# Local attention with the values as the stationary operand of four column groups and the mask in row tiles

## The chip, the cores and the metric

The kernel runs on one core of a Trainium2 chip. The metric is the device time of one execution in microseconds, the median over several runs. TensorE multiplies matrices from SBUF into PSUM, VectorE (DVE) and ScalarE (ACT) read and write both memories, GpSimd (POOL) works on SBUF only, and SyncE (SP) issues the DMAs. The engines run their own instruction streams and wait for each other by semaphores.

## The reference, cut to what matters

Two transformer blocks with adaptive layer norm run over x of shape (4, 1024, 256). The change touches only the attention of the first block, a local one with 16 heads of 16 channels and a window of 64 keys:

```python
h, w, dh, p = 16, 64, 16, 32
q = (x @ Wq.T).reshape(b, l, h, dh)
xp = jnp.pad(x, ((0, 0), (p, p), (0, 0)))
k = (xp @ Wk.T).reshape(b, l + 2 * p, h, dh)
v = (xp @ Wv.T).reshape(b, l + 2 * p, h, dh)
win_idx = jnp.arange(l)[:, None] + jnp.arange(w)[None, :]
scores = jnp.einsum('blhd,blwhd->blhw', q, k[:, win_idx]) * dh ** -0.5
attn = jax.nn.softmax(scores, axis=-1)
out = jnp.einsum('blhw,blwhd->blhd', attn, v[:, win_idx]).reshape(b, l, d)
return out @ Wo.T + bo
```

Query l sees keys l to l + 63 of the padded sequence. Four more stages follow: a latent attention, a mixture of experts, a rotary attention and a second mixture of experts. The change leaves them alone.

## The kernel before, in words

`windowed_attention` (L448) handles 4 batches of 1024 tokens. Each batch has 16 windows (NWIN) of 64 queries; a window needs the 128 keys around its queries, so 64 slots s = 0 to 63 of the main loop stand for the windows of all batches, and w is the slot's place in its batch. The 16 heads go in 8 pairs of 32 channels: the query tile `qm` holds each pair's 64 queries twice, once with the first head's channels and once with the second's (the others zeroed by `parity`), so one matmul per pair gives 128 rows (two heads by 64 queries) of 128 keys.

A window passes through these steps:

- `score` (L820): the mask `bandb` (bf16, 128 x 128) goes into the four PSUM banks of `S` by an identity matmul, one per bank (L827). Then eight matmuls of 32 rows each add the scores (L834), the four row tiles of the array in turn, each into its own bank. A plain fp32 matmul shows as two instructions in the trace, so there are sixteen.
- `softmax` (VectorE, L579): the row maximum of all 1024 columns (L581), then the subtraction into `D` (L585). The next window's `score` waits for the subtraction (`shifted`), since `S` is there once. ScalarE takes the exponential (L750).
- `turn_p` (L840): eight transposes of `D` (L846), copied to `PTs` by ScalarE (L757).
- `weigh` (L850): per pair the transposed weights `PTs` are the stationary operand (128 columns) and the pair's 32 value channels with two columns of ones move (34 columns, L862). Row sums come out beside the values. Both heads' rows meet both heads' channels, and only half of the products is wanted.
- `normal_out` (VectorE, L589): reciprocal of the sums (L592), its masking by `own` (L594), and the product that scales the values and zeroes the unwanted half (L599) into `Yn`.
- `lay` (L866): a selector product with `sel` folds the two heads' rows together and transposes (L871). `lay_out` (VectorE, L603) copies the result to `yT` (L608).

Odd windows read the values from `Vodd`, a copy of `V` shifted by 64 tokens, that two DMAs on SP's queue make per batch (L523, L524).

Beside the windows go **turns**: pieces of work on one shared PSUM bank. Those of a batch's preparation are four transposes of the normalised input ("turn"), four projections each for "query" and "key" (six fp32r matmuls of 512 columns, L799) and five for "value" (L809); ScalarE empties them. An "out" turn is the output projection of four windows (eight instructions of 256 columns, L816); VectorE adds the bias (`output`, L618), and GpSimd multiplies by the gate and adds to x (L694, L697). For the first batch the preparation comes ahead of the loop. For the others, and for all outputs, `WindowPlan` (L399) gives each slot at most two turns, and all of them use one bank, `PJ`. In a slot TensorE goes through this order (end of `windowed_attention`, L884 on):

```python
turn_p(s); lay(s - 2); score(s + 2); turn_bank(turns[0]); weigh(s - 1); turn_bank(turns[1])
```

and VectorE through `lay_out(s - 2)`, `softmax(s + 2)`, `normal_out(s - 1)`, then in slots 0 to 5 of batches 0 to 2 a piece of the next batch's layer norm (four BN_STATS in w = 0, four and eight aggregations in w = 1, four normalisations L576 in each of w = 2 and 3, two low parts `tokens_low` L626 in each of w = 4 and 5), then `output` where the slot has an out turn. An out turn for windows up to 4u + 3 stands in slot 4u + 6 (OUT_AT), as the first turn of its slot; the preparation begins in w = 3.

Of the kernel before, what the change touches and what calls it, by code (L numbers as in the profile page):

```python
# [14 lines left out]
P = 128  # L15
# [383 lines left out]
class WindowPlan:  # L399
# [9 lines left out]
    OUT_AT, FIRST_AT = 6, 3  # L409
    FIRST_BANKS = 6  # L410

    def __init__(self):
# [3 lines left out]
        self.slots = {}  # L416
        for s in range(B * NWIN + 3):
            b, i = divmod(s - self.OUT_AT, 4)
            out = [("out", b // 4, b % 4)] if i == 0 and 0 <= b < 4 * B else []
            self.slots[s] = out  # L420
        for b in range(1, B):
            s = (b - 1) * NWIN + self.FIRST_AT
            for kind, u in self.HEAD:
                while len(self.slots[s]) >= 2:
                    s += 1
                self.slots[s].append((kind, b, u))
        for s in sorted(self.slots):
            for turn in self.slots[s]:
                self.take(turn, self.FIRST_BANKS)
# [18 lines left out]
def windowed_attention(nc, sems, X, MODT, ROWS, ident, identb, eps, W, K):  # L448
    plan = WindowPlan()
    SLOTS = B * NWIN  # L450
    with ExitStack() as ctx:
# [8 lines left out]
        band, bandb = sb("band", [P, P]), sb("bandb", [P, P], BF16)  # L460
        parity = sb("parity", [P, 2])
        own = sb("own", [P, 2])
        sel = sb("sel", [P, WINDOW])
# [11 lines left out]
        V = sb("V", [P, 2, TT + 1, PAIRS, 34])  # L475
        Vodd = sb("Vodd", [P, 2, TT, PAIRS, 34])
# [3 lines left out]
        r = sb("r", [P, 2, PAIRS])  # L480
        rm = sb("rm", [P, 2, PAIRS, 2])
        Yn = sb("Yn", [P, 2, PAIRS, 2, A_DH])
# [7 lines left out]
        Y = O[:, 3 * P:3 * P + KC * WINDOW]  # L490
# [10 lines left out]
        recip, normal, laid, laid_out = signal("recip"), signal("normal"), signal("laid"), signal("laid_out")  # L501
# [10 lines left out]
        def _(sp):  # L512
# [6 lines left out]
            def odd_values(b):  # L519
                sp.wait_ge(freed_a, plan.after(("value", b, 4)))  # L520
                if b >= 2:
                    sp.wait_ge(weighed, NWIN * (b - 1))
# [11 lines left out]
            for dst, src in ((parity, K["parity"]), (band, K["band"]), (own, K["own"]), (sel, K["sel64"])):  # L534
                sp.dma_start(dst[:, :], src).then_inc(wload, 16)
# [22 lines left out]
        def _(v):  # L558
# [1994 lines left out]
```

## Time and profile before

| | us |
|---|---|
| median of three runs | 3053.94 |
| lowest, highest | 3047.06, 3055.08 |
| the profiled execution's own time | 3045.3 |
| its span | 3043.5 |

The profiler records one execution. A span is the time from its first to its last instruction. TensorE is busy for 86% of it, its weight loads for 70%, VectorE for 57%, ScalarE for 41%, GpSimd for 25%. A group of instructions is named by line, engine, operation and tiles; local attention's tiles begin with `w_`. Busy times of TensorE's matmuls overlap, so that the distance from start to start says what an instruction costs in a stream. "x16" is a run of sixteen merged into one row. In brackets stands how long the engine was idle before, and what released it. The granted clock (PEclk) is a share of full speed.

### The profile page before, as it was taken

The numbers are of one execution on the slowest core, as the hardware profiler recorded it, in microseconds if no ns is written. First come the engines' busy times: TensorE is split into PE (matmuls) and PEld (weight loads), VectorE is DVE, ScalarE is ACT, GpSimd is POOL, SyncE is SP. The second block draws the span as 40 slices with busy tenths as digits, with TensorE's granted clock in tenths as the row PEclk, the third lists the DMA queues.
The fourth block names the chain that finished last, engine by engine and source line by source line (L and its number), as shares of the span: only waits on it lengthen the run. The fifth ranks groups of instructions, "written<-read, shape, count | busy, mean of one in ns | idle before, by whom it ended". The sixth has DMA issues, their size and how long they took to land. (4 is left out here: it accounts for less than half of the span.)

```text
span 3043.5 us, 42168 instructions
## 1 busy us (share of the span) xinstructions
PE 2623.1 (86%) x15448; PEld 2115.3 (70%) x15448; DVE 1749.3 (57%) x3153; ACT 1248.0 (41%) x1815; POOL 763.3 (25%) x858
## 2 busy tenths in 40 slices
PE   4699998378999899999999939999587666899998
PEld 3588887256777777777777738888455444788887
DVE  3556655257767776687667625665323334666664
ACT  0444443136666566656666623332122113323322
POOL 0011101324343434353433211111133332100100
PEclk8899999679999999999999969999798887999999
DMA  3200100234333333433334222100100003000000
GB/s 119 81 26 24 28 26 15 68 99 120 102 97 109 107 102 98 134 92 103 106 109 112 76 83 77 37 30 15 68 14 16 29 29 116 8 23 8 30 8 15
DMA packets 127091, 194.59 MB, mean 64 GB/s; under 512 B 34864, under 2 KB 93104, under 8 KB 122224
## 3 DMA queue, kind: packets, MB, share of 16 engines
q1 hardware_dynamic: 125104, 191.50, 21.0%
q8 instruction: 118, 1.93, 0.3%
q10 hardware_dynamic: 1792, 0.53, 0.1%
q14 instruction: 77, 0.63, 0.1%
HBM read 118.28 MB, written 61.34 MB: 59 GB/s over the span
## 5 line engine op out<-in xcount | busy, mean ns | idle before, releaser
L1251 DVE TENSOR_REDUCE l_negmax<-l_mx 128x1 f32<-128x512 f32 (+3 forms) x608 | 393.7, 653 | 144.6 <-PE l_mx L1600 143.9
L1481 ACT ACTIVATE l_Phi<-l_s 128x1024 fp32r<-128x1024 f32 x288 | 295.1, 1025 | 263.6 <-PE l_s L1620 252.1
L1263 DVE TENSOR_TENSOR l_Plo<-l_s,l_Phi 128x1024 fp32r<-128x1024 f32 x288 | 349.7, 1214 | 13.5 <-ACT l_s L1485 12.8
L1631 PE MATMUL l_o<-l_Phi,l_V 128*128 128x256 f32 x1152 | 309.0, 290 | 7.0 <-ACT l_Osb L1493 2.2
L1618 PE MATMUL l_s<-l_QA,l_KK 128*128 128x512 f32 x576 | 284.6, 494 | 27.3 <-DVE l_Plo L1263 22.7
L1631 PE MATMUL l_o<-l_Plo,l_V 128*128 128x256 f32 x1152 | 302.2, 284 | 0.0
L1600 PE MATMUL l_mx<-l_KK,l_QA 128*128 128x512 f32 (+3 forms) x768 | 274.7, 398 | 29.3 <-DMA l_QB<-l_qd 15.9
L1485 ACT ACTIVATE l_s<-l_s 128x1024 f32<-128x1024 f32 x288 | 295.3, 1025 | 0.0
L2255 ACT ACTIVATE m_hidhi<-m_h 128x512 fp32r<-128x512 f32 x168 | 106.2, 632 | 458.0 <-DVE m_h L2113 458.0
L1631 PEld LDWEIGHTS l_o<-l_Phi,l_V 128*128 128x128 f32 x1152 | 221.6, 192 | 43.0 <-issue 31.7
L1620 PE MATMUL l_s<-l_QB,l_KL 65*128 65x512 f32 x576 | 230.8, 401 | 0.0
L1631 PEld LDWEIGHTS l_o<-l_Plo,l_V 128*128 128x128 f32 x1152 | 220.9, 192 | 13.2
L2358 PE MATMUL m_a<-m_wdhi,m_hidhi 128*128 128x256 f32 x672 | 214.5, 319 | 4.8 <-DVE m_tmp L2098 4.5
L1395 POOL TENSOR_TENSOR l_Y<-l_Osb,l_R 64x512 f32<-64x512 f32 x128 | 163.8, 1280 | 175.5 <-DMA l_R<-l_rd 166.6
L2358 PE MATMUL m_a<-m_wdhi,m_hidlo 128*128 128x256 f32 x672 | 189.9, 283 | 0.0
L2358 PE MATMUL m_a<-m_wdlo,m_hidhi 128*128 128x256 f32 x672 | 189.3, 282 | 0.0
L2117 DVE TENSOR_TENSOR m_hidlo<-m_h,m_hidhi 128x512 fp32r<-128x512 f32 x168 | 120.3, 716 | 107.4 <-ACT m_hidhi L2255 107.4
L2105 DVE TENSOR_TENSOR m_sg<-m_sg,m_c 128x512 f32<-128x512 f32 x128 | 87.7, 685 | 161.2 <-PE m_c L2346 143.5
L1600 PEld LDWEIGHTS l_mx<-l_KK,l_QA 128*128 128x128 f32 x768 | 143.3, 200 | 48.8 <-DMA l_QB<-l_qd 18.5
L1376 POOL TENSOR_TENSOR l_rp<-l_rp,l_cos 128x256 f32<-128x256 f32 x64 | 46.8, 732 | 492.2 <-DMA l_rps<-l_rp 481.1
L1618 PEld LDWEIGHTS l_s<-l_QA,l_KK 128*128 128x128 f32 x576 | 111.4, 193 | 61.0 <-DVE l_Plo L1263 40.4
L2205 POOL TENSOR_TENSOR m_xb<-m_xb,m_tmp 128x256 f32<-128x256 f32 x64 | 54.7, 871 | 342.1 <-DVE m_tmp L2098 339.6
(344 smaller groups left out, 6049.1 us busy)
## 6 DMA issues: line engine op xcount, KB each, us to landing
l_qd<-l_qs SPq DMA_DIRECT2D x256, 128.0 KB, 2.4
l_QA<-l_qd SPq DMA_DIRECT2D x64, 512.0 KB, 4.5
l_QB<-l_qd SPq DMA_DIRECT2D x64, 256.0 KB, 5.2
l_R<-l_rd SPq DMA_DIRECT2D x128, 128.0 KB, 3.0
l_rps<-l_rp SPq DMA_DIRECT2D x128, 64.0 KB, 1.9
m_xb<-xs SPq DMA_DIRECT2D x8, 1024.0 KB, 4.8
w_Vodd<-w_V SPq DMA_DIRECT2D x8, 544.0 KB, 5.6
w_xb<-in_x SPq DMA_DIRECT2D x4, 1024.0 KB, 6.1
```

The source lines that it names most:

```text
L1251: v.tensor_reduce(negmax[:, n % 2, at + h0:at + h1], piece_of(number, chunk), AX.X, ALU.max, negate=True).then_inc(reduced, 1)
L1263: v.tensor_tensor(Plo[:, s % 3].rearrange("p u h q -> p (u h q)"), S2[s % 2][:, :], Phi[:, s % 3].rearrange("p u h q -> p (u h q)").bitcas ...
L1395: g.tensor_tensor(Y[rows, quad % 2, 2 * grp:2 * grp + 2].rearrange("p j t q -> p t j q"), Osb[rows, r % 3, :, odd * 2 * P:(odd + 1) * 2 * ...
L1481: a.activation(Phi[:, s % 3].rearrange("p u h q -> p (u h q)"), S2[s % 2][:, :], ACT.Exp, scale=L_D ** -0.5).then_inc(exped, 1)
L1485: a.activation(S2[s % 2][:, :], S2[s % 2][:, :], ACT.Exp, scale=L_D ** -0.5).then_inc(exped, 1)
L1600: mm = pe.matmul(bank[:, h - h0, :], QA[:, n % 4, h, t, :], KK[:, b % 2, k0 * P:k1 * P], start=not diagonal, stop=(h == h1 - 1), skip_grou ...
L1618: pe.matmul(bank, KK[:, b % 2, k * P:(k + 1) * P], QA[:, m % 4, :, t, :], start=not diagonal, stop=False, skip_group_check=diagonal)
L1620: pe.matmul(bank, KL[:, b % 2, k * P:(k + 1) * P], QB[:, m % 4, :, t, :], start=False, stop=True, skip_group_check=diagonal).then_inc(scor ...
L1631: mm = pe.matmul(O[:, odd * 2 * P:(odd + 1) * 2 * P].rearrange("p (j q) -> p j q", j=2), V[:, b % 2, k, 64 - 64 * odd:192 - 64 * odd], src ...
L2117: v.tensor_tensor(hidlo[:, n % 3, :], h[:, n % 2, :], hidhi[:, n % 3, :].bitcast(F32), ALU.subtract).then_inc(low, 1)
L2255: a.activation(hidhi[:, n % 3, :], h[:, n % 2, :], ACT.Copy).then_inc(high, 1)
L2358: mm = pe.matmul(acc[q // 2][:, (q % 2) * C:(q % 2 + 1) * C], x[:, n % 3, q * P:(q + 1) * P], w[:, j, :], start=(j == 0 and q % 2 == 0 and ...
```

## The change

The values become the stationary operand. For each pair, `weigh` loads the pair's 32 value channels (32 columns) and streams the 128 columns of `PTs`, so that the output comes already transposed, channels on partitions. The four pairs of a group go to the four column groups of the array and write partitions 0 to 31, 32 to 63, 64 to 95 and 96 to 127 of the bank `O`. A second set of matmuls with 32 columns of ones gives the sums, spread over the same partitions. That makes 16 matmuls, 32 instructions, per window. `normal_out` picks each channel's own head by `parity` in two passes over 256 columns, takes the reciprocal of the 128 sums of each partition, and multiplies 128 elements into `yT`. `lay`, `lay_out`, `Yn`, `own` and `sel` are gone, and with them one slot of delay.

The mask goes in as eight matmuls of 32 rows: `hot` has the rows' one-hot of the query within each half of 32 queries, `pen` the penalties. `V` and `Vodd` lose the columns of ones. An out turn stands one slot earlier (OUT_AT 5) and is last in its slot. So slot 5 is (query, out) where it was (query, key), 6 is (key, query) where it was (out, query), 9 is (key, out), 10 and 11 are (value, value), 12 is (value), 13 and 17 are (out) alone, and likewise 16 slots on.

```diff
-    OUT_AT, FIRST_AT = 6, 3
+    OUT_AT, FIRST_AT = 5, 3
     FIRST_BANKS = 6
 
     def __init__(self):
         self.index, self.bank, self.order = {}, {}, []
         for n, (kind, u) in enumerate(self.HEAD):
             self.take((kind, 0, u), n % self.FIRST_BANKS)
-        self.slots = {}
-        for s in range(B * NWIN + 3):
-            b, i = divmod(s - self.OUT_AT, 4)
-            out = [("out", b // 4, b % 4)] if i == 0 and 0 <= b < 4 * B else []
-            self.slots[s] = out
+        last = {self.OUT_AT + 4 * n: ("out", n // 4, n % 4) for n in range(4 * B)}
+        self.slots = {s: [] for s in range(B * NWIN + 2)}
         for b in range(1, B):
             s = (b - 1) * NWIN + self.FIRST_AT
             for kind, u in self.HEAD:
-                while len(self.slots[s]) >= 2:
+                while len(self.slots[s]) + (s in last) >= 2:
                     s += 1
                 self.slots[s].append((kind, b, u))
         for s in sorted(self.slots):
+            if s in last:
+                self.slots[s].append(last[s])
             for turn in self.slots[s]:
...
-        band, bandb = sb("band", [P, P]), sb("bandb", [P, P], BF16)
+        pen, penb = sb("pen", [P, 2, P]), sb("penb", [P, 2, P], BF16)
+        hot, hotb = sb("hot", [P, 2, P]), sb("hotb", [P, 2, P], BF16)
+        ones = sb("ones", [P, 32])
...
-        own = sb("own", [P, 2])
-        sel = sb("sel", [P, WINDOW])
...
-        V = sb("V", [P, 2, TT + 1, PAIRS, 34])
-        Vodd = sb("Vodd", [P, 2, TT, PAIRS, 34])
+        V = sb("V", [P, 2, TT + 1, C])
+        Vodd = sb("Vodd", [P, 2, TT, C])
...
-        r = sb("r", [P, 2, PAIRS])
-        rm = sb("rm", [P, 2, PAIRS, 2])
-        Yn = sb("Yn", [P, 2, PAIRS, 2, A_DH])
+        part, both = sb("part", [P, 2, 2, WINDOW]), sb("both", [P, 2, 2, WINDOW])
+        r = sb("r", [P, 2, WINDOW])
...
-            for dst, src in ((parity, K["parity"]), (band, K["band"]), (own, K["own"]), (sel, K["sel64"])):
-                sp.dma_start(dst[:, :], src).then_inc(wload, 16)
+            sp.dma_start(parity[:, :], K["parity"]).then_inc(wload, 16)
+            for dst, src in ((pen, K["pen"]), (hot, K["hot"])):
+                sp.dma_start(dst[:, :, :], src).then_inc(wload, 16)
...
             def normal_out(n):
-                o3 = O[:, 0:PAIRS * 34].rearrange("p (n d) -> p n d", d=34)
-                v.wait_ge(weighed, n + 1)
-                v.reciprocal(r[:, n % 2, :], o3[:, :, 32]).then_inc(recip, 1)
-                v.wait_ge(recip, 2 * n + 1)
-                v.tensor_tensor(rm[:, n % 2], r[:, n % 2, :, None].broadcast_to([P, PAIRS, 2]),
-                                own[:, None, :].broadcast_to([P, PAIRS, 2]), ALU.mult).then_inc(recip, 1)
-                v.wait_ge(recip, 2 * n + 2)
-                if n >= 2:
-                    v.wait_ge(laid, n - 1)
-                v.tensor_tensor(Yn[:, n % 2], o3[:, :, 0:32].rearrange("p n (h d) -> p n h d", h=2),
-                                rm[:, n % 2, :, :, None].broadcast_to([P, PAIRS, 2, A_DH]), ALU.mult)\
-                    .then_inc(normal, 1)
-
-            def lay_out(n):
                 b, w = divmod(n, NWIN)
-                v.wait_ge(laid, n + 1)
+                x = O[:, :].rearrange("p (x g h q) -> p x g h q", x=2, g=2, h=2)
+                v.wait_ge(weighed, 4 * n + 4)
+                v.tensor_scalar(part[:, :, :, :], x[:, :, :, 0, :], parity[:, 0:1], None, ALU.mult).then_inc(picked, 1)
+                v.wait_ge(picked, 2 * n + 1)
+                v.scalar_tensor_tensor(both[:, :, :, :], x[:, :, :, 1, :], parity[:, 1:2], part[:, :, :, :],
+                                       ALU.mult, ALU.add).then_inc(picked, 1)
+                v.wait_ge(picked, 2 * n + 2)
+                v.reciprocal(r[:, :, :], both[:, 1]).then_inc(recip, 1)
+                v.wait_ge(recip, n + 1)
                 if b >= 1 and w % 4 == 0:
                     v.wait_ge(freed_v, plan.after(("out", b - 1, w // 4)))
-                v.tensor_copy(yT[:, :, w * WINDOW:(w + 1) * WINDOW], Y.rearrange("p (k q) -> p k q", k=KC))\
+                v.tensor_tensor(yT[:, :, w * WINDOW:(w + 1) * WINDOW], both[:, 0], r[:, :, :], ALU.mult)\
                     .then_inc(laid_out, 1)
...
-                v.memset(V[:, b, :, :, 32:34], 1.0).then_inc(consts, 1)
...
-            v.wait_ge(wload, 9 * 16)
-            v.tensor_copy(bandb[:, :], band[:, :]).then_inc(consts, 1)
+            v.wait_ge(wload, 8 * 16)
+            v.tensor_copy(penb[:, :, :], pen[:, :, :]).then_inc(consts, 1)
+            v.tensor_copy(hotb[:, :, :], hot[:, :, :]).then_inc(consts, 1)
+            v.memset(ones[:, :], 1.0).then_inc(consts, 1)
...
-            for s in range(SLOTS + 3):
+            for s in range(SLOTS + 2):
                 b, w = divmod(s, NWIN)
-                if 2 <= s < SLOTS + 2:
-                    lay_out(s - 2)
                 if s + 2 < SLOTS:
                     softmax(s + 2)
...
-                    n, rows = (1, P) if u == 4 else (2, P)
-                    a.activation(V[0:rows, b % 2, 2 * u:2 * u + n, :, 0:32],
-                                 bank[0:rows, 0:n * C].rearrange("p (t n d) -> p t n d", t=n, d=32), ACT.Copy)\
-                        .then_inc(freed_a, 1)
+                    n = 1 if u == 4 else 2
+                    a.activation(V[:, b % 2, 2 * u:2 * u + n, :].rearrange("p t c -> p (t c)"), bank[:, 0:n * C],
+                                 ACT.Copy).then_inc(freed_a, 1)
...
-                for q in range(4):
-                    pe.matmul(S[:, q * HALF:q * HALF + 2 * P], identb[:, :],
-                              bandb[:, None, :].broadcast_to([P, 2, P]), start=True, stop=False,
-                              skip_group_check=True)
+                for half in range(2):
+                    for q in range(4):
+                        rows = slice(32 * q, 32 * q + 32)
+                        pe.matmul(S[:, q * HALF:q * HALF + 2 * P], hotb[rows, half, :],
+                                  penb[rows, half, None, :].broadcast_to([32, 2, P]), start=(half == 0), stop=False,
+                                  skip_group_check=True)
...
                 pe.wait_ge(copied, 2 * n + 2)
                 if n >= 1:
-                    pe.wait_ge(normal, n)
-                    pe.wait_ge(laid_out, n)
+                    pe.wait_ge(picked, 2 * n)
                 if w == 0:
                     pe.wait_ge(freed_a, plan.after(("value", b, 4)))
                 elif w == 1:
                     pe.wait_ge(odd[b % 2], 32 * (b // 2 + 1))
                 values = Vodd if w % 2 else V
-                for i in range(PAIRS):
-                    mm = pe.matmul(O[:, i * 34:(i + 1) * 34], PTs[:, n % 2, i * P:(i + 1) * P],
-                                   values[:, b % 2, w // 2, i, :], start=True, stop=True)
-                mm.then_inc(weighed, 1)
-
-            def lay(n):
-                pe.wait_ge(normal, n + 1)
-                if n >= 1:
-                    pe.wait_ge(laid_out, n)
-                for k in range(KC):
-                    mm = pe.matmul(Y[:, k * WINDOW:(k + 1) * WINDOW],
-                                   Yn[:, n % 2, 4 * k:4 * k + 4].rearrange("p n h d -> p (n h d)"),
-                                   sel[:, :], start=True, stop=True)
-                mm.then_inc(laid, 1)
-
-            pe.wait_ge(wload, 9 * 16)
+                for g in range(2):
+                    for x in range(2):
+                        for q in range(4):
+                            i = 4 * g + q
+                            weights = ones[:, :] if x else values[:, b % 2, w // 2, i * 32:(i + 1) * 32]
+                            mm = pe.matmul(O[32 * q:32 * q + 32, x * sums + g * P:x * sums + (g + 1) * P], weights,
+                                           PTs[:, n % 2, i * P:(i + 1) * P], start=True, stop=True,
+                                           skip_group_check=True)
+                            if g == x == 1:
+                                mm.then_inc(weighed, 1)
...
-            for s in range(SLOTS + 3):
+            for s in range(SLOTS + 2):
                 turns = plan.slots[s]
                 if s < SLOTS:
                     turn_p(s)
-                if 2 <= s < SLOTS + 2:
-                    lay(s - 2)
                 if s + 2 < SLOTS:
                     score(s + 2)
...
-    q = i % WINDOW
-    off = i[None, :] - q[:, None]
-    k["band"] = np.where((off >= 0) & (off < WINDOW), 0, MASKED).astype(f)
+    q = 32 * np.arange(2)[None, :, None] + i[:, None, None] % 32
+    off = i[None, None, :] - q
+    k["pen"] = np.where((off >= 0) & (off < WINDOW), 0, MASKED).astype(f)
+    k["hot"] = (i[None, None, :] % WINDOW == q).astype(f)
     k["parity"] = (i[:, None] // A_DH % 2 == np.arange(2)[None, :]).astype(f)
-    k["own"] = (i[:, None] // WINDOW == np.arange(2)[None, :]).astype(f)
-    k["sel64"] = (q[:, None] == np.arange(WINDOW)[None, :]).astype(f)
```

## Rows read from the trace of the kernel before

**Rows 1.** Stretches: busy us (count) of PE, PEld, DVE, ACT, POOL; clock; DMA share; GB/s.

```profile
119.00:522.00 403.00, 372.57 (x3482) 329.07 (x3482) 253.25 (x487) 174.74 (x266) 45.88 (x62) 0.98 0.09 24
```

**Rows 2.** Waits of that stretch: waiter <- releaser: total us, times, longest.

```profile
DVE w_m L581 <- PE w_s L834: 69.7, 59, 18.7
...
DVE w_yT L608 <- PE w_o L871: 63.4, 41, 5.5
```

**Rows 3.** Timeline of one plain slot: start us, us, engine, line, operation.

```profile
319.85 0.66 PE L871 MATMUL w_o<-w_sel,w_Yn 128*128 128x64 f32 x4
...
320.34 0.60 PE L827 MATMUL w_s<-w_bandb,identb 128*128 128x256 bf16 x4
...
320.87 0.54 PEld L834 LDWEIGHTS w_s<-w_kT,w_qm 32*128 32x128 f32 x16 [0.21 <-issue]
...
321.53 1.97 PE L862 MATMUL w_o<-w_V,w_PT 128*128 128x34 f32 x16
321.75 1.22 DVE L581 TENSOR_REDUCE w_m<-w_s 128x8 f32<-128x1024 f32 x1 [0.91 <-PE w_s L834]
323.00 1.22 DVE L585 TENSOR_TENSOR w_D<-w_s,w_m 128x1024 f32<-128x1024 f32 x1
323.23 0.94 PEld L846 LDWEIGHTS w_t<-ident,w_D 128*128 128x128 f32 x8
323.34 1.07 PE L846 MATMUL w_t<-ident,w_D 128*128 128x128 f32 x8
324.14 0.20 DVE L592 RECIPROCAL w_r<-w_o 128x8 f32<-128x8 f32 x1
...
324.58 0.42 DVE L599 TENSOR_TENSOR w_Yn<-w_o,w_rm 128x256 f32<-128x256 f32 x1
...
325.06 0.66 PE L871 MATMUL w_o<-w_sel,w_Yn 128*128 128x64 f32 x4 [0.65 <-DVE w_Yn L599]
...
326.96 1.22 DVE L581 TENSOR_REDUCE w_m<-w_s 128x8 f32<-128x1024 f32 x1 [0.91 <-PE w_s L834]
```

**Rows 4.** Timeline, slot 6 and the slot after it.

```profile
159.09 1.23 DVE L581 TENSOR_REDUCE w_m<-w_s 128x8 f32<-128x1024 f32 x1 [0.91 <-PE w_s L834]
...
164.20 0.50 PE L799 MATMUL w_pj<-w_hThi,w_wqhi 128*128 128x512 f32 x1 [1.63 <-DVE w_tmp L618]
...
166.36 1.91 PE L846 MATMUL w_t<-ident,w_D 128*128 128x128 f32 x8
...
169.98 1.22 DVE L581 TENSOR_REDUCE w_m<-w_s 128x8 f32<-128x1024 f32 x1 [0.91 <-PE w_s L834]
...
177.11 1.23 DVE L581 TENSOR_REDUCE w_m<-w_s 128x8 f32<-128x1024 f32 x1 [0.91 <-PE w_s L834]
```

**Rows 5.** VectorE groups by shape, whole kernel: busy us, mean ns of one.

```profile
L273 DVE RECIPROCAL r_rs<-r_sums 128x1 f32<-128x1 f32 x32 | 4.9, 153 | 0.0
...
L2026 DVE RECIPROCAL m_red<-m_red 128x8 f32<-128x8 f32 x8 | 1.6, 203 | 0.3
...
L2027 DVE TENSOR_TENSOR m_comb<-m_comb,m_red 128x128 f32<-128x128 f32 x4 | 1.2, 292 | 0.1
```

**Rows 6.** Timeline, VectorE, at the stage's start and end.

```profile
122.93 1.23 DVE L581 TENSOR_REDUCE w_m<-w_s 128x8 f32<-128x1024 f32 x1 [2.40 <-PE w_s L834]
...
126.89 1.23 DVE L581 TENSOR_REDUCE w_m<-w_s 128x8 f32<-128x1024 f32 x1 [1.47 <-PE w_s L834]
...
139.35 1.37 DVE L576 TENSOR_SCALAR w_xn<-w_xb,w_mv,w_rstd 128x256 f32<-128x256 f32 x4
...
513.77 1.22 DVE L581 TENSOR_REDUCE w_m<-w_s 128x8 f32<-128x1024 f32 x1 [0.91 <-PE w_s L834]
```

**Rows 7.** Timeline, the last two output turns.

```profile
517.59 1.95 PE L816 MATMUL w_pj<-w_wo,w_yT 128*128 128x256 f32 x8
...
537.45 0.76 DVE L618 TENSOR_TENSOR w_tmp<-w_pj,w_bo 128x256 f32<-128x256 f32 x2 [3.61 <-PE w_pj L816]
```

**Rows 8.** Table of stretches, slot 0 (columns as in rows 1).

```profile
126.89:130.84 3.95, 2.48 (x30) 1.92 (x30) 3.76 (x7) 2.02 (x4) 0.00 (x0) 1.00 0.02 4
```

More of the change, by code:

```diff
@@ L489, in windowed_attention @@
         banks = [S[:, i * HALF:(i + 1) * HALF] for i in range(4)] + [TR[0][:, :], TR[1][:, :], PJ[:, :]]
-        Y = O[:, 3 * P:3 * P + KC * WINDOW]
+        sums = 2 * P
         wload, consts = signal("wload"), signal("consts")
@@ L500, in windowed_attention @@
         turned, copied, weighed = signal("turned"), signal("copied"), signal("weighed")
-        recip, normal, laid, laid_out = signal("recip"), signal("normal"), signal("laid"), signal("laid_out")
+        picked, recip, laid_out = signal("picked"), signal("recip"), signal("laid_out")
         gated, added = signal("gated"), signal("added")
@@ L521, in odd_values @@
                 if b >= 2:
-                    sp.wait_ge(weighed, NWIN * (b - 1))
+                    sp.wait_ge(weighed, 4 * NWIN * (b - 1))
                 sp.dma_start(Vodd[0:64, b % 2], V[64:128, b % 2, 0:TT]).then_inc(odd[b % 2], 16)
@@ L740, in evacuate @@
                     if b >= 2 and u == 0:
-                        a.wait_ge(weighed, NWIN * (b - 1))
+                        a.wait_ge(weighed, 4 * NWIN * (b - 1))
                         a.wait_ge(odd[b % 2], 32 * (b // 2))
-                    n, rows = (1, P) if u == 4 else (2, P)
-                    a.activation(V[0:rows, b % 2, 2 * u:2 * u + n, :, 0:32],
-                                 bank[0:rows, 0:n * C].rearrange("p (t n d) -> p t n d", t=n, d=32), ACT.Copy)\
-                        .then_inc(freed_a, 1)
+                    n = 1 if u == 4 else 2
+                    a.activation(V[:, b % 2, 2 * u:2 * u + n, :].rearrange("p t c -> p (t c)"), bank[:, 0:n * C],
+                                 ACT.Copy).then_inc(freed_a, 1)
             def exp(n):
@@ L755, in copy_turned @@
                     if g == 0 and n >= 2:
-                        a.wait_ge(weighed, n - 1)
+                        a.wait_ge(weighed, 4 * n - 4)
                     a.activation(PTs[:, n % 2, g * HALF:(g + 1) * HALF], TR[g][:, :], ACT.Copy).then_inc(copied, 1)
             masked, tokens = signal("masked"), signal("tokens")
-            a.wait_ge(wload, 9 * 16)
+            a.wait_ge(wload, 8 * 16)
             for n, (w, hi) in enumerate(((wq, wqhi), (wk, wkhi), (wv, wvhi))):
@@ L860, in weigh @@
                 values = Vodd if w % 2 else V
-                for i in range(PAIRS):
-                    mm = pe.matmul(O[:, i * 34:(i + 1) * 34], PTs[:, n % 2, i * P:(i + 1) * P],
-                                   values[:, b % 2, w // 2, i, :], start=True, stop=True)
-                mm.then_inc(weighed, 1)
-            def lay(n):
-                pe.wait_ge(normal, n + 1)
-                if n >= 1:
-                    pe.wait_ge(laid_out, n)
-                for k in range(KC):
-                    mm = pe.matmul(Y[:, k * WINDOW:(k + 1) * WINDOW],
-                                   Yn[:, n % 2, 4 * k:4 * k + 4].rearrange("p n h d -> p (n h d)"),
-                                   sel[:, :], start=True, stop=True)
-                mm.then_inc(laid, 1)
-            pe.wait_ge(wload, 9 * 16)
+                for g in range(2):
[8 more added lines that the diff above has]
+                                mm.then_inc(weighed, 1)
+            pe.wait_ge(wload, 8 * 16)
             pe.wait_ge(consts, 12)
@@ L881, in _ @@
             score(1)
-            for s in range(SLOTS + 3):
+            for s in range(SLOTS + 2):
                 turns = plan.slots[s]
```

## The prediction

> **What bounds the kernel now.** I began with the table of stretches, to find the stage: the local attention's 64 windows run from about 119 to 522 us of the span, with TensorE busy for 373 of 403 us, VectorE for 253 and a granted clock of 0.98 [rows 1]. Next the waits of that stage: VectorE waits 70 us for the scores and 63 us for the selector product [rows 2]. Then the timeline of one window slot without extra work [rows 3], which shows a loop and not one busy engine. The reduction starts at 321.75, the subtraction follows, then the reciprocal, its mask and `Yn` (324.14 to 325.00); only then may TensorE run the selector product (325.06), mask and scores, and the next reduction starts at 326.96. The loop is 5.21 us: 2.47 of softmax, 0.9 of normalising, 1.8 of TensorE. TensorE's own work is 0.94 (transposes) + 0.49 (selector) + 0.53 (mask) + 0.66 (scores) + 1.81 (values) = 4.4 us, so it has little slack. With two projection turns of six matmuls it is the bound: such a slot takes 7.13 us (169.98 to 177.11), 2.7 us over its plain work, 0.23 a matmul [rows 4]. The third kind is the slot where an output turn comes first and a query turn second: both use the one bank PJ, TensorE stands 1.63 us until VectorE has emptied it, the clock drops and eight transposes take 1.91 instead of 1.07 us; 10.9 us from one reduction (159.09) to the next [rows 4]. There are six slots of that order (slots 6 and 10 of batches 0 to 2).
>
> **The change, TensorE.** The selector product (four instructions, 0.49) and its place in the loop go. The mask: now eight instructions of 32 rows, four row tiles at a time. Today four take 0.53 with 0.21 of standing before the first score [rows 3]; about 0.107 each, so eight at four abreast take 0.21. The scores show what row tiles give: sixteen 128-column instructions in 0.66, where sixteen at the transposes' pace (0.94 for eight, 0.117 each) would take 1.9. I read 0.66 as a quarter of that, 0.45, and 0.2 for draining, the same 0.2 as ahead of the scores. The values: today sixteen loads of 128 columns at 0.113 (1.81). New: 32 instructions, each with 128 moving fp32 columns, 0.117 long. No row shows column groups. Lower bound: the pace of the row tiles, 32 x 0.117 / 4 = 0.94. Upper bound: one after another, 3.74. I take 0.94, since the nearest row is the score row, also fp32 with tiles in turn. Switches of tile shape: 0.2 each, three in a plain slot (transposes to mask, scores to values, values to transposes), a fourth where a turn lies between. TensorE per slot: 0.94 + 0.2 + 0.21 + 0.45 + 0.2 + 0.94 + 0.2 = 3.15; with two projections + 12 x 0.23 + 0.2 = 6.15.
>
> **The change, VectorE.** Gone: reciprocal of 8 and its mask (0.44 from 324.14 to 324.58), `Yn` (0.42), the copy of 128 elements to `yT` (about 0.3). New, each waiting for the one before it: two passes over 256 PSUM elements (like `Yn`, 0.42, start to start 0.45), a reciprocal of 128 elements, a product of 128 elements (0.29 [rows 5]). The reciprocal is the surprise: one element takes 153 ns, eight take 203 [rows 5], so 7.1 ns an element more, where a product of 128 elements takes 292 in all. 203 + 120 x 7.1 = 1.05 us. Bounds: 0.29, priced like the product, and 3.2, if all of the 203 ns grew with the count; I take 1.05, since two sizes of the same operation give it. The Trainium skill (VectorE: DVE Perf Modes, "First, the fixed hardware budget") gives reciprocal a repeat count of 8, which at about 1.04 ns a pass (the product's 128 elements against the reduction's 1024) would be an estimate of 1.2 us, and 7 us more in the total.
> VectorE per slot: 1.26 + 1.14 + 0.45 + 0.45 + 1.08 + 0.21 = 4.6 us (start to start, as in rows 3; an instruction that does not depend on its forerunner starts some 0.08 before its end). Mask and scores now start as soon as the subtraction ends and take 1.2 until the reduction can start, under the 2.2 of normalising. So the loop is cut, and VectorE alone becomes the bound of a plain slot: 4.6 for 5.21. The score loop by itself would be 3.7; it is 3.96 today at the start of the stage (122.93 to 126.89), where nothing is normalised [rows 6].
>
> **Slot by slot**, from the second reduction of the stage to the 64th (126.89 to 513.77, 386.9 us [rows 6]). Slots 0 to 4 of batches 0 to 2 carry VectorE work of the next batch, about 1.4 us (four instructions, 1.37 [rows 6]) and 2.2 in slot 1: 6.0 in slots 0, 2 and 3, 5.9 in slot 4. That is *worse* than the loop of 5.21, whose waits for TensorE (0.91 a slot before the reduction [rows 3]) take up most of such work today. Slot 1 now also holds an output turn: 8.4 (its values and then the normalising wait for 1.95 us of output matmuls [rows 7]; 6.75 in batch 0, which has none there). Slot 5 (query, output) 7.2; slot 6 6.7, since its key turn waits for late token remainders; 7 and 8 6.15; 9 (key, output) 6.5; 10 and 11 6.2; 12, 14, 15 4.6; 13 (output alone, ahead of the values, for which the normalising waits) 6.2. Sum 97.4; batch 0, whose first slot has nothing to normalise, 93.7; the last 13 slots 10 x 4.6 + 3 x 6.2 = 64.6. Total 353.1: **33.8 us less**. The six slots of the wrong order (10.9 against 6.7 in slot 6) and the plain ones carry it.
> The tail, from the last softmax to the last output turn's end, is 23.7 us now (513.77 to 537.45 [rows 6, 7]) with three rounds of values, selector, copy; new: 2.5 softmax, 1.1 exp, then values and normalising of windows 61 to 63 close together, output at about 16.7: **7 us less**. Start: 160 KB more of constants, one DMA less, two casts for one: **0.8 more**. SP's queue carries no wait of the change except the load count; GpSimd's adds move one slot earlier and have slack. The clock: a plain slot leaves TensorE 1.4 us without work. In a stretch where it was busy 2.48 of 3.95 us the clock was still 1.00 [rows 8], but a 1.63 us pause cost one drop [rows 4]. I add **4 us**: a few cold stretches of some 4 us at the entry to the full slots.
> Sum: -33.8 - 7 + 0.8 + 4 = -36. The profiled execution took 3045.3 us (span 3043.5), so 3009 by it; the median of the runs is 8.6 above it, so 3054 - 36 = **3018**.
>
> **The rivals.** (1) *The reciprocal is cheap*, 0.29: 40 VectorE-bound slots and the tail gain 0.76 each, 32 us: 2986. For it: every other VectorE operation here costs about 1 ns an element. Against: rows 5.
> (2) *Values only half abreast*: the columns' weight loads (32 columns, a quarter of 0.113) stand between the matmuls, 32 x 0.028 = 0.9 more, a values step of 1.85, as now. Hidden behind VectorE in plain slots; it counts in 21 full slots, in 8 with an output turn ahead, and in the tail: 28 us, 3046. Against: the transposes load and stream the whole array at 0.117, so a load does hide behind a matmul of the same rows. A clock that stays low in plain slots would cost about 15 us, between this and the forecast.
> (3) *The column groups run one after another*: the values take 3.74 us. The mechanism is this one step; all normalising waits for it. Plain slots 6.2, full ones 9.0, preparing ones 7.6: 19 x 6.2 + 6 x 8.2 + 29 + 11 x 7.6 + 3.9 + 21 x 9.0 + 6 = 478 for 386.9, with the tail +94: **3148, slower**. It decides from a values step of about 2.1 us on, where the savings are used up. For it: no row shows a column group. Against: the score rows. It is also the case that the change does not do what it says.
>
> **How the numbers follow.** Forecast 0.64, rival 1 0.10, rival 2 0.15, rival 3 0.11. The range takes in rivals 1 and 2: 2984 to 3050; the forecast's own, with the reciprocal from 0.8 to 1.3 us and the clock's cost from 0 to 15, is 3000 to 3035. 0.3% (9 us) is about what can be told from no change here; rival 2 ends at that edge, half of it counts as no change. Faster 0.81, same 0.08, slower 0.11.
>
> **What would show it.** Right: a plain slot of 4.6 us from reduction to reduction, no idle time of VectorE before it; 32 values instructions within about 1 us; a reciprocal near 1.05; slots 0 to 4 longer than before, slots 6 and 10 near 6.5; no wait of a turn for `tmp`. Wrong: values over 2 us, a reciprocal near 0.3, a granted clock under 0.9 in the stage, or TensorE pauses over 0.3 at each change of tile shape.

## The result and the profile after

| | before | after |
|---|---|---|
| median, us | 3051.5 (4 runs) | 3014.3 (4 runs, 3009.4 to 3017.8) |
| ratio, 95% interval | | 0.988, 0.986 to 0.990 |
| span of the profiled execution | 3043.5 | 3015.4 |
| local attention, first load to the next stage's first load | 468.2 | 432.2 |
| third to 64th reduction (slots 0 to 60) | 386.9 | 356.2 |

The forecast was 3018 us, in a range of 2984 to 3050. The third row says less than the others: the stages that the change does not touch took 2575.3 us in the profiled execution before and 2583.2 in the one after (span less the fourth row), and between 2568 and 2591 over all kernels of this study. So the experiments below are read by the fourth row first; it fell by 36.0 us. There is one profile of each kernel, so how well that row repeats was not measured. Within a profile, slots with the same work mostly agree to 0.02 us from batch to batch; those in which the clock falls do not.

The stretch of the changed kernel from slot 0 to the last reduction, by the table of stretches (columns as in [rows 1]), and then the waits from 119 to 490 us, counterpart of [rows 2]. It starts at 127.60, the third reduction of the stage, as 126.89 is in the kernel before; the prediction calls this one the second, and its 61 slots are counted from there all the same.

```profile
127.60:483.77 356.17, 287.08 (x4338) 228.93 (x4338) 309.80 (x474) 171.12 (x259) 45.93 (x62) 0.92 0.09 25
```

```profile
PE w_s L820 <- DVE w_D L584: 41.5, 24, 3.7
DVE w_m L580 <- PE w_s L827: 37.5, 21, 18.3
DVE w_part L592 <- PE w_o L858: 22.6, 18, 3.5
```

VectorE is busy 310 of 356 us now and TensorE 287: the two have changed places. VectorE's wait for the selector product is gone, its wait for scores is about halved (69.7 to 37.5 us, 18 of each a single wait at the start), a wait of 22.6 us for the values is new, and what TensorE waits for is VectorE's subtraction (the mask, L820, is the first matmul that needs it). The granted clock went from 0.98 to 0.92.

A plain slot of the changed kernel, by the timeline, counterpart of [rows 3]:

```profile
430.03 1.22 DVE L580 TENSOR_REDUCE w_m<-w_s 128x8 f32<-128x1024 f32 x1
431.28 1.23 DVE L584 TENSOR_TENSOR w_D<-w_s,w_m 128x1024 f32<-128x1024 f32 x1
432.43 0.47 DVE L592 TENSOR_SCALAR w_part<-w_o,w_parity 128x256 f32<-128x256 f32 x1
...
432.57 0.40 PE L820 MATMUL w_s<-w_penb,w_hotb 32*128 32x256 bf16 x8 [1.51 <-DVE w_D L584]
...
432.80 0.61 PE L827 MATMUL w_s<-w_kT,w_qm 32*128 32x128 f32 x16
432.94 0.48 DVE L594 SCALAR_TENSOR_TENSOR w_both<-w_o,w_parity,w_part 128x256 f32<-128x256 f32 x1
433.45 0.95 DVE L597 RECIPROCAL w_r<-w_both 128x128 f32<-128x128 f32 x1
...
433.57 0.43 PE L858 MATMUL w_o<-w_PT,w_Vodd 128*32 128x128 f32 x8 [0.16 <-DVE w_both L594]
...
433.78 0.43 PE L858 MATMUL w_o<-w_PT,w_ones 128*32 128x128 f32 x8
...
434.44 0.29 DVE L601 TENSOR_TENSOR w_yT<-w_both,w_r 128x128 f32<-128x128 f32 x1
434.58 0.86 PEld L839 LDWEIGHTS w_t<-ident,w_D 128*128 128x128 f32 x8 [0.20 <-issue]
434.58 1.09 PE L839 MATMUL w_t<-ident,w_D 128*128 128x128 f32 x8
434.65 1.22 DVE L580 TENSOR_REDUCE w_m<-w_s 128x8 f32<-128x1024 f32 x1
```

Read VectorE first: 430.03, 431.28, 432.43, 432.94, 433.45, 434.44, 434.65. There is no bracket on any of its lines, so it does not wait in this slot, and the slot is the sum of its six instructions, 4.62 us (5.21 before). TensorE waits 1.51 us for the subtraction, and its work from the mask to the start of the next transposes is 432.57 to 434.58. Values and ones come in four runs of eight, 0.21 to 0.22 apart: 32 instructions in 0.87 us.

Slots 5 and 6 of the changed kernel, counterpart of [rows 4]. The output turn now ends slot 5:

```profile
159.71 1.99 PE L807 MATMUL w_pj<-w_wo,w_yT 128*128 128x256 f32 x8 [0.35 <-ACT w_qm L721]
...
161.54 1.04 PE L839 MATMUL w_t<-ident,w_D 128*128 128x128 f32 x8
...
163.62 1.21 DVE L580 TENSOR_REDUCE w_m<-w_s 128x8 f32<-128x1024 f32 x1
163.75 0.50 PE L790 MATMUL w_pj<-w_hThi,w_wkhi 128*128 128x512 f32 x1 [0.40 <-DVE w_tmp L611]
...
169.83 1.23 DVE L580 TENSOR_REDUCE w_m<-w_s 128x8 f32<-128x1024 f32 x1 [0.94 <-PE w_s L827]
...
175.65 1.23 DVE L580 TENSOR_REDUCE w_m<-w_s 128x8 f32<-128x1024 f32 x1 [0.93 <-PE w_s L827]
```

Transposes, mask and scores stand between the output and the next turn on PJ, so TensorE waits 0.40 us for `tmp` (the forecast had no such wait) and not 1.63, the clock stays up (transposes in 1.04), and slot 6 takes 6.21 us where it took 10.89. The slot after it takes 5.82 (7.13).

VectorE's groups in the local attention, counterpart of [rows 5]:

```profile
L597 DVE RECIPROCAL w_r<-w_both 128x128 f32<-128x128 f32 x61 | 58.1, 953 | 2.1
L594 DVE SCALAR_TENSOR_TENSOR w_both<-w_o,w_parity,w_part 128x256 f32<-128x256 f32 x61 | 29.5, 484 | 2.2
L592 DVE TENSOR_SCALAR w_part<-w_o,w_parity 128x256 f32<-128x256 f32 x61 | 29.3, 480 | 24.3 <-PE w_o L858 22.6
```

The place that came out most differently from the forecast is the last batch. A lone output turn there, in slot 53, by the timeline:

```profile
437.04 0.48 DVE L592 TENSOR_SCALAR w_part<-w_o,w_parity 128x256 f32<-128x256 f32 x1
...
439.27 1.22 DVE L580 TENSOR_REDUCE w_m<-w_s 128x8 f32<-128x1024 f32 x1
...
439.50 3.40 PE L807 MATMUL w_pj<-w_wo,w_yT 128*128 128x256 f32 x8 [1.47 <-DVE w_yT L601]
...
444.26 0.48 DVE L592 TENSOR_SCALAR w_part<-w_o,w_parity 128x256 f32<-128x256 f32 x1 [2.52 <-PE w_o L858]
```

The reduction at 439.27 is followed by eight output matmuls that take 3.40 us where [rows 7] have 1.95, so they run at the lower level of 1.2 GHz. TensorE had stood 1.47 us for `yT`, and VectorE then stands 2.52 us for values that queue behind them. Slots 49, 53 and 57 took 8.89, 7.89 and 8.89 us; slots 13, 29 and 45, of the same make but behind fuller slots, 6.25. The same happened in slots 17 and 33, which also follow slots without turns of their own. In slot 17:

```profile
224.45 3.39 PE L807 MATMUL w_pj<-w_wo,w_yT 128*128 128x256 f32 x8 [1.47 <-DVE w_yT L601]
```

So the output matmuls ran at half clock in five of the eight slots with a lone output turn from slot 13 to slot 57 (3.39 to 3.75 us), and at full clock in the other three (1.96 to 1.97 us).

### The profile page after: what moved, and what is told of

It is laid out like the page before. It is cut to its first block and busy times, and to the rows that moved or that the text cites. A ratio compares the mean times of both kernels' runs of the same rounds, so it can differ in the third digit from the quotient of the medians.

```text
span 3015.4 us, 44082 instructions
## 1 busy us (share of the span) xinstructions
PE 2548.5 (85%) x16472; PEld 2022.8 (67%) x16472; DVE 1820.6 (60%) x3153; ACT 1249.7 (41%) x1815; POOL 762.6 (25%) x858
```

## The experiments

All are small edits of one of the two kernels. The fourth row of the table above is called the stage. A ratio is to the median of the kernel before, run beside the experiment on the same chip, with its 95% interval. Most of these ratios are within 2% of 1, so the profiles' slots have to carry the argument.

**The order of the turns alone, in the kernel before.**

```diff
-        for s in range(B * NWIN + 3):
-            b, i = divmod(s - self.OUT_AT, 4)
-            out = [("out", b // 4, b % 4)] if i == 0 and 0 <= b < 4 * B else []
-            self.slots[s] = out
+        last = {self.OUT_AT + 4 * n: ("out", n // 4, n % 4) for n in range(4 * B)}
+        self.slots = {s: [] for s in range(B * NWIN + 3)}
```

> The kernel before with one part of the change alone: an output turn that shares its slot comes last in it (still one slot later than in the change). If the gain has two sources, the cut loop and the order on bank PJ, only slots 6 and 10 of batches 0 to 2 shorten, from 9.3 to 12.1 us to about 7.1 each; together 19 us less, so 3032. Plain slots stay at 5.21. If the whole gain were the order of turns, it would come near 3014; if the order were hidden, it stays at 3051.

Measured: 3039.6 us, ratio 0.998 (0.996 to 1.000), stage 454.4, 13.8 shorter. The six slots went from 61.8 us in all to 44.8 (7.45 to 7.50 each), plain slots stayed 5.22. One slot (1) took 7.53 for 5.34 and gave 2.2 back. The part is smaller than the 19 us expected, and it is not the whole gain.

**The old order in the changed kernel.** The plan of before, with OUT_AT 6.

> The changed kernel with the old plan of turns (output turns in slot 4n + 6 and first in their slot). If the order is worth about as much here as in the kernel before, slots 6 and 10 take some 9 us again (TensorE waits for VectorE, which now also has a longer normalising ahead of the bias), and the kernel about 3030; plain slots stay 4.62. If the cut loop carries everything: 3014. The lone output turns no longer wait for yT, which may give back up to 5 us.

Measured: 3026.4 us, ratio 0.992 (0.989 to 0.995), stage 444.3, 12.1 longer than the changed kernel's. Slot 6, by the timeline:

```profile
163.73 1.23 DVE L581 TENSOR_REDUCE w_m<-w_s 128x8 f32<-128x1024 f32 x1
...
169.70 0.50 PE L791 MATMUL w_pj<-w_hThi,w_wqhi 128*128 128x512 f32 x1 [3.18 <-DVE w_tmp L612]
...
171.43 1.91 PE L840 MATMUL w_t<-ident,w_D 128*128 128x128 f32 x8
...
174.76 1.23 DVE L581 TENSOR_REDUCE w_m<-w_s 128x8 f32<-128x1024 f32 x1 [5.12 <-PE w_s L828]
```

The wait for `tmp` is 3.18 us, twice that of [rows 4], because the bias stands behind the longer normalising (166.66 to 168.89 by the same timeline); the transposes run at half the clock again, and the slot takes 11.03. The six slots take 68.1 us for 36.4. But the lone output turns, one slot later, no longer wait for `yT`: 5.28 us in slots 50, 54 and 58, where the changed kernel has 8.89, 7.89 and 8.89 in the slots before. So the 12 us are what the new plan as a whole, order and place, is worth here. The six slots lose 32 us by the old plan, and the other slots give some 17 back, 10 of them in the last batch; up to 5 were expected from the lone output turns. Placing these one slot earlier thus cost much of what the order brought.

**The full-array mask in the changed kernel.** Four identity matmuls with `bandb` again, nothing else.

> The changed kernel with the mask as four full-array matmuls again. TensorE gets some 0.35 us more in each slot. If VectorE bounds plain and preparing slots and TensorE only the 21 slots 5 to 11, it costs 21 x 0.35 = 7 us, 3022, with plain slots still at 4.62. If the mask is in a loop everywhere, it costs 64 x 0.35 = 22 us, 3036.

Measured: 3016.4 us, ratio 0.989 (0.985 to 0.993), stage 429.3: 2.9 us *shorter* than the changed kernel's. The slots explain it. Plain slots are 4.62, as expected; slots 7 and 8 are 6.15 for 5.84, so 0.3 us lost in each TensorE-bound slot, also as expected. Slots 5 to 11 of the three batches lose 5.7 us together. But slots 49, 53 and 57 are 6.25, 6.26 and 6.24 and slot 17 is 7.25 for 8.54: the clock no longer falls there. Over the last batch, the changed kernel and then this one, by the table of stretches (PEclk is the third number from the end):

```profile
400.00:483.80 83.80, 58.14 (x1014) 45.03 (x1012) 72.06 (x103) 31.86 (x47) 11.45 (x16) 0.90 0.04 14
```

```profile
400.00:482.00 82.00, 61.60 (x1017) 47.38 (x1015) 76.20 (x108) 34.28 (x50) 11.47 (x16) 1.00 0.10 27
```

This does not separate the two candidates, the wait and the light load of TensorE, since the longer mask also shortens the wait for `yT`, from 1.47 to 1.05 us. And it is no rule: in slot 33 the output matmuls still ran at half clock, behind the same wait of 1.05. Slots 49 and 33, in this order:

```profile
422.69 1.97 PE L804 MATMUL w_pj<-w_wo,w_yT 128*128 128x256 f32 x8 [1.05 <-DVE w_yT L599]
```

```profile
324.72 3.51 PE L804 MATMUL w_pj<-w_wo,w_yT 128*128 128x256 f32 x8 [1.05 <-DVE w_yT L599]
```

**The column groups one after another.**

```diff
-                for g in range(2):
-                    for x in range(2):
-                        for q in range(4):
+                for q in range(4):
+                    for g in range(2):
+                        for x in range(2):
```

> The changed kernel with the values' matmuls in another order: all eight instructions of a column group before the next group's. The arithmetic is the same. If the 0.86 us of the 32 instructions come from four column groups working side by side, they now take about 3.4 us (32 x 0.107), plain slots about 6, and the kernel about 3014 + 120 = 3134 (the slow rival of the prediction). If the pace comes from short loads and streams alone, nothing changes: 3014.

Measured: 3058.2 us, ratio 1.003 (1.001 to 1.005), stage 472.9, 40.7 longer. The values of one window, by the timeline of TensorE's matmuls:

```profile
471.46 0.38 PE L858 MATMUL w_o<-w_PT,w_V 128*32 128x128 f32 x2 [0.16 <-DVE w_both L594]
471.68 0.38 PE L858 MATMUL w_o<-w_PT,w_ones 128*32 128x128 f32 x2
471.89 0.41 PE L858 MATMUL w_o<-w_PT,w_V 128*32 128x128 f32 x4
472.11 0.41 PE L858 MATMUL w_o<-w_PT,w_ones 128*32 128x128 f32 x4
472.36 0.41 PE L858 MATMUL w_o<-w_PT,w_V 128*32 128x128 f32 x4
...
473.51 0.38 PE L858 MATMUL w_o<-w_PT,w_ones 128*32 128x128 f32 x2
```

A run of two instructions (one fp32 matmul in one column group) takes 0.215 us, the same as a run of eight in four groups above: side by side, four groups cost what one costs. The whole step takes 2.2 us and not 3.4, as the runs of four show: at each change of group the last two matmuls of one group run beside the first two of the next, ten steps and not sixteen. So the direction was right and the size a third of the expected: without the side-by-side work the kernel is slower than before. Plain slots were expected at about 6 us and stay at 4.62, although this values step is longer than the 1.8 us of before: there the gain over 5.21 is the cut loop's alone. The pace of the values counts where TensorE is the bound: slots 7 and 8 take 7.2 us here, 5.8 in the changed kernel and 7.1 before.

This kernel also holds the wait for `yT` as it is in the changed kernel and gives TensorE more work around it. Slot 49, and the last batch by the table of stretches:

```profile
460.64 1.97 PE L807 MATMUL w_pj<-w_wo,w_yT 128*128 128x256 f32 x8 [1.47 <-DVE w_yT L601]
```

```profile
439.00:524.50 85.50, 76.06 (x1056) 64.93 (x1056) 74.68 (x105) 32.94 (x48) 11.51 (x16) 1.00 0.06 18
```

The wait of 1.47 us stands ahead of the output turns of slots 17, 33, 49, 53 and 57 alike, and all of them run at full clock (slots 49, 53 and 57 take 7.52). So the wait alone does not bring the clock down; it does so where TensorE had little work around it.

**The lone output turns behind the values**, in the changed kernel.

```diff
-                if turns:
-                    turn_bank(turns[0])
+                early = [t for t in turns[:1] if t[0] != "out"]
+                for turn in early:
+                    turn_bank(turn)
                 if 1 <= s <= SLOTS:
                     weigh(s - 1)
-                if len(turns) > 1:
-                    turn_bank(turns[1])
+                for turn in turns[len(early):]:
+                    turn_bank(turn)
```

> The changed kernel with an output turn that is alone in its slot put behind the values' matmuls, not ahead of them. It tests the account of the 8.9 us slots 49, 53 and 57 of the changed kernel: TensorE stands 1.5 us for yT, the clock falls to half, and the normalising waits for output matmuls and values at the low clock. If so, these slots fall to about 5.4 us (4.62 + 0.75 of VectorE's bias), slots 13, 29, 45 from 6.25 to 5.4, 17 and 33 from 8.5 to 7.4; stage 15 us shorter, kernel about 2999. If the low clock comes from the low load of TensorE in plain slots alone, the slots stay near 8 us and the gain is under 5 us.

Measured: 3001.4 us, ratio 0.985 (0.983 to 0.987), stage 415.7, 16.5 shorter than the changed kernel's; 15 were expected. Slots 49, 53 and 57 take 5.28 to 5.29, slots 13, 29 and 45 the same, 17 and 33 7.24. TensorE in slot 49:

```profile
412.51 1.96 PE L807 MATMUL w_pj<-w_wo,w_yT 128*128 128x256 f32 x8 [0.28 <-DVE w_yT L601]
```

With 0.28 us in place of 1.47 none of the eight lone output turns runs at half clock, though TensorE has no more work than in the changed kernel. The clock does fall once behind such a turn, hidden: from 421.11 four runs of values are 0.43 apart, and the slot is still 4.62.

**A copy in place of the reciprocal**, in the changed kernel: `v.tensor_copy` for `v.reciprocal`.

> The changed kernel with a copy of 128 elements in place of the reciprocal; it leaves the division by the softmax sums out. If VectorE bounds the plain and the preparing slots, about 40 slots lose 0.95 - 0.29 = 0.66 us each, plain ones 3.96, stage 26 us shorter, kernel about 2988 (rival 1 of the prediction, measured). If the loop of the scores is the bound, plain slots do not go under 4.6.

Measured: 2971.1 us, ratio 0.975 (0.973 to 0.977), stage 390.4, 41.8 shorter. Plain slots take 3.89 to 3.90, most of the preparing slots 0 to 4 lose 0.5 to 0.7 each (slots 18 and 34 nothing), and the TensorE-bound slots 7 and 8 stay 5.84. The surplus of 16 us over the 26 lies largely with the clock: slots 49, 53 and 57 take 5.53 (3.4, 2.4 and 3.4 less) and slots 17 and 33 6.51 (2.0 less each), with the wait for `yT` down to 0.74 us and these output turns at full clock. Another 5 us lie outside the 61 slots.

**Full-array mask and late lone outputs together.**

> The changed kernel with the full-array mask and the lone output turns behind the values. If the row-tiled mask saves 0.3 us in the 21 TensorE-bound slots and its one drawback was the clock in slots 49, 53 and 57, then with the output turns late the row-tiled mask must win: this one is 6 to 7 us slower in the stage than the kernel with the late output turns alone. If the row tiles lower the clock elsewhere too, the two are alike.

Measured: 3004.7 us, ratio 0.985 (0.983 to 0.987), stage 420.4, 4.7 more than with the row-tiled mask, where 6 to 7 were expected. Every slot from 5 to 11 is longer by 0.1 to 0.3 and the rest is nearly equal: once the output turns do not meet a falling clock, the row-tiled mask is worth these 5 us.

**VectorE's chain spread**, in the changed kernel: ScalarE takes the first pick, GpSimd the product, `both` and `r` are there twice.

```diff
-                v.tensor_scalar(part[:, :, :, :], x[:, :, :, 0, :], parity[:, 0:1], None, ALU.mult).then_inc(picked, 1)
+                a.activation(part[:, :, :, :], x[:, :, :, 0, :], ACT.Copy, scale=parity[:, 0:1]).then_inc(halved, 1)
...
-                v.tensor_tensor(yT[:, :, w * WINDOW:(w + 1) * WINDOW], both[:, 0], r[:, :, :], ALU.mult)\
+                g.tensor_tensor(yT[:, :, w * WINDOW:(w + 1) * WINDOW], both[:, n % 2, 0], r[:, n % 2], ALU.mult)\
```

> The changed kernel with the first picking pass on ScalarE and the last product on GpSimd, both with time to spare. VectorE's chain drops by 0.52 + 0.21 us to 3.9. If VectorE's own time is the bound, plain slots take 3.9, some 40 slots gain 0.7 each, 28 us, kernel about 2988, less whatever a lower clock takes back since TensorE then has 3.2 us of work in 3.9. If the latency between the engines matters instead, plain slots stay over 4.3.

Measured: 2978.0 us, ratio 0.975 (0.973 to 0.978), stage 397.9, 34.3 shorter than the changed kernel's. Plain slots take 3.71 to 3.80, even under the 3.9 expected and far from the 4.3 at which passing work between engines would have mattered. The lone outputs are 6.38 to 6.39.

**Both gaining steps together, and the same with the full-array mask.**

> Both steps that gained, together: lone output turns behind the values, first pick on ScalarE, last product on GpSimd. The lone output slots fall from 6.39 to about 4.5 us (3.72 + 0.75 for the bias), 17 and 33 from 7.1 to about 6; stage 324.2 - 13 = 311 us, kernel about 2965. If TensorE's clock falls in plain slots of 3.72 us with a late output turn, less.

Measured: 2971.0 us, ratio 0.974 (0.972 to 0.976), stage 384.9, 47.2 shorter than the changed kernel's and 83 shorter than before. Plain slots 3.71 to 3.81, lone outputs 4.53 to 4.54, 17 and 33 6.34; third to 64th reduction 311.8 (the 324.2 and 311 of the expectation are this stretch). One slot from reduction to reduction by VectorE's timeline, without a wait:

```profile
419.37 1.16 DVE L581 TENSOR_REDUCE w_m<-w_s 128x8 f32<-128x1024 f32 x1
420.56 1.23 DVE L585 TENSOR_TENSOR w_D<-w_s,w_m 128x1024 f32<-128x1024 f32 x1
421.70 0.48 DVE L594 SCALAR_TENSOR_TENSOR w_both<-w_o,w_parity,w_part 128x256 f32<-128x256 f32 x1
422.22 0.95 DVE L597 RECIPROCAL w_r<-w_both 128x128 f32<-128x128 f32 x1
423.09 1.16 DVE L581 TENSOR_REDUCE w_m<-w_s 128x8 f32<-128x1024 f32 x1
```

> The same with the full-array mask. TensorE then has 3.5 us of work in plain slots of 3.72, and the score loop is longer by 0.3: plain slots about 3.95 and the 21 full slots 0.3 longer each; 15 us slower than with the row-tiled mask, about 2980. If the mask's row tiles only matter where TensorE is the bound: 2971.

Measured: 2980.7 us, ratio 0.977 (0.976 to 0.979), stage 397.7, 12.7 more. Plain slots 3.95, the score loop's own length as in [rows 6], TensorE-bound ones 6.16. Now the mask counts in nearly every slot: the shorter the loop, the more it is worth.

## Why the prediction was right, point by point

**The loop.** Right. A plain slot was forecast at 4.6 us with VectorE as its bound; it is 4.62, VectorE's six instructions have no wait in them, and the copy in place of the reciprocal takes its whole 0.7 us out of the slot. The slot stays at 4.62 even with a values step of 2.2 us.

**The terms of VectorE.** The reciprocal was taken at 1.05 us and took 0.953; (953 - 203) / 120 = 6.2 ns an element beyond the eighth, where [rows 5] gave 7.1. The two picks were taken at 0.42 and took 0.48. The errors cancel. The estimate of 1.2 us from the repeat count that the Trainium skill gives (VectorE: DVE Perf Modes) was 0.25 too high. An element beyond the eighth costs 6.2 ns, six times the product's 1.04, so the trace agrees in kind, not with the count of 8. Rival 1, a cheap reciprocal, is measured: it would have given a stage 42 us shorter. That is more than the 32 us of the forecast, largely because the clock then did not fall in the lone output slots.

**The terms of TensorE.** Values 0.94 forecast, 0.87 measured, so the pace of the row tiles holds for column groups. The changes of tile shape, taken at 0.2 us each, were priced too high. In a TensorE-bound slot, from 167.86 us on, where nothing on TensorE waits, the steps from start to start are 0.97 for the transposes, 0.23 for the mask, 0.54 for the scores and 1.01 for the values; the forecast's terms with their switches are 1.14, 0.21, 0.65 and 1.14. That is why such slots take 5.83 us and not 6.15. The rule of the Trainium skill (TensorE: Matmul & The Clock Gate, "What overlaps and what doesn't" in Part 3) by which loads would stand between matmuls of the same row group, rival 2, does not show: 32 loads and 32 matmuls share 0.87 us, as fast as in the row tiles. Rival 3 did not come true for the order of loops in the change, but its mechanism exists: in the other order the values take 2.2 us and the kernel is slower than before by 0.3%, close to the 2.1 us at which the prediction put the turn. A full 3.74 us did not come about in either order, since even then neighbouring groups overlap, and at 2.2 us the plain slots did not lengthen.

**The slots.** Forecast against measured: slots 0 and 2 6.0 and 5.9; 4 5.9 and 5.8; 5 7.2 and 7.1; 6 6.7 and 6.2; 7 and 8 6.15 and 5.8; 9 6.5 and 6.2; 10 and 11 6.2 and 5.9; 12, 14 and 15 4.6 and 4.6; 13 6.2 and 6.25; 17 8.4 and 8.5. Slot 17 agrees by luck: the forecast had its output matmuls at 1.95 us, they took 3.39, and with them at full clock the slot takes 7.25 (the full-array mask). So its term was 1.2 us too high, and the clock made up for it. Preparing slots did get longer, 5.9 for 5.2. Slot 3 is the exception, 6.85 for 6.0; the clock over the 17 us that hold it in batch 0 is 0.70:

```profile
137.90:155.00 17.10, 11.67 (x164) 9.38 (x168) 15.93 (x27) 9.59 (x14) 1.91 (x2) 0.70 0.01 1
```

Over slots 2 and 3 of batches 0, 1 and 2 the granted clock is 0.60, 0.60 and 0.73, where the kernel before has 1.00 in each. Slot 3 keeps 6.5 us in the spread kernel, so not all of it need be the clock; what share is was not measured. The sum was 353.1 and is 356.2.

**The clock, the term that was mis-sized and in the main misplaced.** I had put 4 us at the entry to the full slots. There, in slot 3 of three batches, it cost at most 2.6 (3 x 0.85). It cost about 7 in slots 49, 53 and 57 (25.7 us for 3 x 6.25) and 2.5 in slots 17 and 33 (17.0 for 2 x 7.25). The step that failed is the one on lone output turns: "output alone, ahead of the values ... 6.2". It holds in slots 13, 29 and 45 and not where slots without turns go before, since the turn's wait for `yT`, which the earlier place brings, comes on top of a lightly loaded TensorE. Removing the wait (late lone outputs, 5.28 us) ends it, and so does more work on TensorE at the same wait of 1.47 us (the column groups one after another, these output turns at 1.97). The full-array mask changes both a little and ends it in four of the five slots, not in slot 33. What exactly brings the clock down stays open.

**The tail and the start.** 7 us less were forecast for the tail and 4.7 came (483.77 to 502.71 = 18.9 us): its last output turn runs at half clock, 3.75 us. The one of before did so too (533.99, 3.42 us), which [rows 7] do not show, and the forecast did not say at which clock it took the new one. The start was to cost 0.8 more; from the first load to the third reduction it is 48.1 us for 48.6. So the stage fell by 36.0 us, the forecast's sum to the tenth, and that is luck, since errors of both signs are in it: 3 us too much gain was forecast in the slots and 2 too much in the tail, against 1.3 too much cost at the start and the clock's 4 us, which are already in the measured slots. Inside the slots too, the TensorE-bound ones were forecast 0.3 us too long and the lone output slots too short. The median fell by 37.2.

**The shares.** The new plan of turns is worth 12 to 14 us of the 36: 13.8 for the order alone in the kernel before, 12.1 for order and place in the changed one. The changed kernel with the old plan has the other 24. The row-tiled mask, as the change has it, gained nothing (-2.9 us by the stage of the kernel without it, one profile of each). So the 24 us are the values' step and the loop without the selector product, which were not separated further, except that plain slots owe nothing to the faster values.

## What to carry to other kernels

When a loop over two engines is cut, the next bound is the sum of one engine's instructions: price each new one by its own kind, and a reciprocal by its element count. Put a turn whose consumer shares a queue with a long chain last in its slot, and one whose input is just being made behind work that is ready. An array tiled by columns paid here only where neighbouring instructions went to different groups; and a saving on TensorE where TensorE is not the bound can come back as a lower clock. A forecast that agrees to the tenth is no proof of its terms: compare them one by one.

## What the runs showed of the hardware

- Eight instructions in four column groups of 32 columns take 0.215 us, as two in one group do. The order of the loops decides between 0.87 and 2.2 us for the same 32.
- A reciprocal of 128 fp32 elements a partition takes 953 ns, a product of as many 292.
- A wait of TensorE of 1.47 us ahead of an output turn went with a fall of the clock from full to half (eight matmuls in 3.40 to 3.75 instead of 1.97 us) in the three slots of the last batch, where TensorE was busy for 58 of 84 us around them. The same wait went with no fall in the same slots when it was busy for 76 of 85.5.
- A halved clock cost nothing where VectorE was the bound: in the kernel with late lone outputs, slot 50 kept its 4.62 us with the values at half pace.
- The stages that no kernel here changed took 2568 to 2591 us in the profiled executions. That is two thirds of the effect studied, so parts of a change were told apart by the stage's own length and the slots'.
